# The last steps of two layers are run inside the layer that follows

## The reference

```python
x = x + mamba(_layernorm(x), ...)
x = x + ffn(_layernorm(x), ...)
x = x + attention(_layernorm(x), ...)
x = x + ffn(_layernorm(x), ...)      # the same expert weights again

# attention, per head of 8 features (16 heads), layernorm first
dist = sqrt(max(q2 + k2 - 2 * Q @ K.T, 0))
W = (SHEP_EPS + dist) ** -2
W = W / (SHEP_EPS + W.sum(-1))
out = X + (G * (W @ V)) @ W_out.T + b_out

# ffn: 16 experts, 8 of them per token, and a shared one
scores = sigmoid(x @ gate_w.T); top 8 of scores + bias, weights normalised and scaled
y = sum over experts of combine_e * ((silu(x @ w_gate_e) * (x @ w_up_e)) @ w_down_e)
y = y + (silu(x @ shared_gate_w) * (x @ shared_up_w)) @ shared_down_w
```

## Time and profile before

| | |
|---|---|
| median of 3 runs | 1519.52 us (1519.46 to 1519.74) |
| the profiled execution | 1515.65 us, span 1513.9 us |
| busy | PE 86%, DVE 84%, ACT 73%, POOL 59% of the span |
| mean granted TensorE clock | 0.899 |

### The profile page before, as it was taken

One profiled execution on the slowest core, in us unless ns is written; L12 is line 12 of the kernel. 1 busy time (PEld: TensorE's weight loads), 2 busy tenths in 40 slices (PEclk: granted clock), 3 DMA queues, 4 the chain that ended last, 5 costly groups with the idle time before them and its releaser, 6 DMA issues. The chain is left out here.

```text
span 1513.9 us, 21515 instructions
## 1 busy us (share of the span) xinstructions
PE 1302.8 (86%) x6448; PEld 636.5 (42%) x6448; DVE 1271.4 (84%) x2150; ACT 1098.4 (73%) x1594; POOL 900.4 (59%) x1054
## 2 busy tenths in 40 slices
PE   4788888998997599999997787788888579999998
PEld 3344445544553244444442233333333234444443
DVE  3999999999999988888886888888878568888885
ACT  4677877786777456556653899999999956656564
POOL 5999889989988666665665232322222026656655
PEclk8999999999999999999998677867666689999999
DMA  7122113111311043322220000000000023333331
GB/s 252 57 73 95 56 56 102 65 56 56 111 56 57 10 166 144 131 112 112 112 112 0 1 1 0 0 0 0 0 0 1 1 113 120 120 119 119 146 155 61
DMA packets 27923, 111.54 MB, mean 74 GB/s; under 512 B 4049, under 2 KB 9570, under 8 KB 19426
## 3 DMA queue, kind: packets, MB, share of 16 engines
q1 hardware_dynamic: 27010, 110.21, 19.4%
q10 hardware_dynamic: 864, 0.74, 0.2%
HBM read 108.06 MB, written 2.88 MB: 73 GB/s over the span
## 5 line engine op out<-in xcount | busy, mean ns | idle before, releaser
L1042 POOL TENSOR_TENSOR e_h_lo<-e_h,e_h_hi 128x512 f16<-128x512 f32 x272 | 314.7, 1158 | 246.4 <-ACT e_h_hi L1124 233.6
L275 POOL TENSOR_TENSOR m_h<-m_b_sb,m_dx 128x512 f32<-128x512 f32 x256 | 347.0, 1383 | 45.6 <-POOLq L67 35.8
L690 DVE TENSOR_TENSOR_SCAN m_h<-m_decay,m_h 128x1024 f32<-128x1024 f32 x112 | 255.9, 2285 | 10.9 <-DVEq L60 7.5
L393 PE MATMUL m_y_ps<-m_hc,ident 128*128 128x512 f32 x512 | 251.1, 614 | 0.0
L528 ACT ACTIVATE m_decay<-m_delta,mw_a_log 128x255 f32<-128x255 f32 x448 | 185.1, 461 | 87.7 <-DVEq L695 87.5
L1119 ACT ACTIVATE e_g<-e_g 128x512 f32<-128x512 f32 x256 | 148.9, 582 | 122.7 <-PE e_g L1064 121.5
L1124 ACT ACTIVATE e_h_hi<-e_h 128x512 f16<-128x512 f32 x272 | 169.7, 624 | 84.6 <-DVE e_h L1175 82.9
L1621 DVE TENSOR_SCALAR a_d<-a_s 128x512 f32<-128x512 f32 x256 | 170.3, 687 | 54.9 <-PE a_s L1508 35.9
L1064 PE MATMUL e_g<-ef_x_hi,ew_gate_up 128*128 128x512 f16 x544 | 207.3, 381 | 4.7 <-PEq L103 3.2
L1069 PE MATMUL e_y<-e_h_hi,ew_down 128*128 128x512 f16 x544 | 205.9, 379 | 2.1 <-POOL e_h_lo L1042 2.1
L1064 PE MATMUL e_u<-ef_x_hi,ew_gate_up 128*128 128x512 f16 x544 | 207.4, 381 | 0.0
(11 more groups left out here) (236 smaller groups left out, 2080.4 us busy)
## 6 DMA issues: line engine op xcount, KB each, us to landing
e_c_rest<-mix SPq DMA_DIRECT2D x48, 1024.0 KB, 8.7
m_b_sb<-b_rows SPq DMA_DIRECT2D x64, 512.0 KB, 5.4
ef_c_head<-mix SPq DMA_DIRECT2D x16, 1024.0 KB, 4.6
ew_gate_up<-w_gate_up SPq DMA_DIRECT2D x1, 2176.0 KB, 13.9
out<-x_sb SPq DMA_DIRECT2D x8, 256.0 KB, 2.3
ew_down<-w_down SPq DMA_DIRECT2D x1, 1088.0 KB, 11.1
mw_conv_rows<-w_conv_rows ACTq DMA_DIRECT2D x1, 640.0 KB
mix<-ef_cT SPq DMA_DIRECT2D x16, 32.0 KB, 1.6
```

The costliest lines, as they stand in the source:

```text
L275: ins = nc.gpsimd.tensor_tensor(h[:, m % 4, :, c], b_sb[:, p, 2 * m:2 * m + 2], dx[:, p, c:c + 1].to_broadcast([P, 2, T]), ALU.mult)
L393: ins = nc.tensor.matmul(y_ps[:], ident[:], hc[:, m % 2, n].rearrange("p c t -> p (c t)"), start=(m == 0 and n == 0), stop=(m == PAIRS - 1 ...
L690: nc.vector.tensor_tensor_scan(flat, decay_of(m, p)[:], flat, 0.0, ALU.mult, ALU.add).then_inc(scan_chain, 1)
L1042: nc.gpsimd.tensor_tensor(h_lo[:, k], h[:, k], h_hi[:, k], ALU.subtract).then_inc(h_lo_ready, 1)
```

## The change

At both seams the last steps of a layer move behind the barrier. `ExpertTail` holds the shared expert's h, its upper and lower half, and y; in layer 1 its last product and the addition now run in the attention's `body(-1)`, at heads 3, 6 and 9. `AttentionTail` holds what the last batch's tail needs; this tail now runs in the steps `e` = 0 to 4 of layer 3's first chunk. The two kinds of layer now share eight PSUM banks, and the first eight experts of that chunk have two banks each for gate and up. The router for this chunk moves one batch earlier (`router`), and the first expert's gate and up are made in the last batch (`first_expert`). GpSimd's norm for batch 1 moves from the attention's start into the last chunk of layer 1, and the Sqrt and Silu tables are asked for ahead. The loops of both layers keep their instructions.

```diff
+class ExpertTail:
...
+    def upper_h(self, act):
+        act.wait_ge(self.h_ready, self.STEPS + 1)
+        act.sem_inc(self.gu_free, 1)
+        self.nc.scalar.activation(self.h_hi[:], self.h[:], ACT.Copy).then_inc(self.h_hi_ready, 1)
+        act.sem_inc(self.h_ready, -(self.STEPS + 1))
+    def lower_h(self, pool):
+        pool.wait_ge(self.h_hi_ready, self.STEPS)
+        self.nc.gpsimd.tensor_tensor(self.h_lo[:], self.h[:], self.h_hi[:], ALU.subtract).then_inc(self.h_lo_ready, 1)
+        pool.sem_inc(self.h_hi_ready, -self.STEPS)
+    def down(self, pe, y):
+        pe.wait_ge(self.h_lo_ready, self.STEPS + 3)
+        for n, (r, a) in enumerate(((0, self.h_hi), (0, self.h_lo), (1, self.h_hi))):
+            ins = self.nc.tensor.matmul(y, self.ew.down[r][:, NE], a[:], start=False, stop=(n == 2))
+        ins.then_inc(self.y_ready, 1)
+        pe.sem_inc(self.h_lo_ready, -(self.STEPS + 3))
+    def read_y(self, act, y):
+        take(act, self.y_ready)
+        self.nc.scalar.activation(self.yT[:], y, ACT.Copy, scale=W_SCALE ** -2).then_inc(self.yT_ready, 1)
+    def transpose_y(self, pe, t):
+        take(pe, self.yT_ready)
+        take(pe, self.gu_free, self.STEPS + self.BANKS)
+        for tt in range(QC // P):
+            ins = self.nc.tensor.transpose(t[:, tt * P:(tt + 1) * P], self.yT[:, tt * P:(tt + 1) * P], self.ident[:])
+        ins.then_inc(self.o_ready, 1)
+    def update(self, dve, t):
+        take(dve, self.o_ready)
+        n = QC // P
+        xs = self.x_sb[:, (NQ - 1) * n:NQ * n, :]
+        self.nc.vector.tensor_tensor(xs, t.rearrange("p (a d) -> p a d", a=n), xs, ALU.add)
...
+        def banks(e, first, last):
+            few = last if nxt is not None else first and e < 8 if prev is not None else False
+            return 2 if few else BANKS
...
+                    if e < NE or not (last and nxt is not None):
+                        lower(e)
...
+                    if e > 0 or not first or prev is None:
+                        up(e, p, first, last)
+                    if first and prev is not None:
+                        prev.tensor_step(pe, e)
...
             def epilogue():
-                for n in range(3):
+                for n in range(2):
                     pe.wait_ge(h_lo_ready, STEPS + n + 1)
                     down(STEPS - 3 + n)
-                pe.sem_inc(h_lo_ready, -(STEPS + 3))
-                take(pe, yT_ready)
-                take(pe, gu_free, STEPS + BANKS)
-                transpose_y()
+                if nxt is None:
+                    rest.down(pe, y_ps)
+                    rest.transpose_y(pe, t_ps)
...
+                    if first and prev is not None:
+                        prev.vector_step(dve, e)
...
-            chunks(dve, body, lambda: None, lambda: update(NQ - 1))
+            chunks(dve, body, (lambda: prev.vector_open(dve)) if prev is not None else (lambda: None), (lambda: update(NQ - 1)) if nxt is None else (lambda: None))
...
+        if e == 12:
+            self.norm(pool)
...
+class AttentionTail:
...
+    def banks_ahead(self):
+        s, av, t, u = self.s_ps, self.av_ps, self.t_ps, self.u_ps
+        return [av[0][:], t[0][:], s[0][:]], [av[1][:], t[1][:], s[1][:]], u[:, 0:512], u[:, 512:1024]
+    def banks_behind(self):
+        s, av, t, u = self.s_ps, self.av_ps, self.t_ps, self.u_ps
+        return [s[0][:], t[0][:], u[:, 0:512]], [s[1][:], t[1][:], u[:, 512:1024]], av[0][:], av[1][:]
...
+    def vector_open(self, dve):
+        self.read_av(dve, 0)
+        self.read_av(dve, 1)
+    def tensor_step(self, pe, e):
+        if e == 1:
+            self.transpose_av(pe)
+        if e == 3:
+            self.transpose_o(pe)
+        if e == 4:
+            self.project_out(pe)
+    def vector_step(self, dve, e):
+        if e == 0:
+            self.norm_and_gate(dve, 1)
+        if e == 2:
+            self.read_oT(dve)
+        if e == 4:
+            self.update(dve, NB - 1)
...
-            body(NB - 2, 0, further=False, ahead=False)
+            body(NB - 2, 0, further=False, ahead=False, router=True)
...
             def prologue():
-                front.norm(pool)
-            def body(b, p, core=True, tail=True, heads=True, ahead=True, further=True, last=False):
-                if last:
-                    experts.norm(pool)
+                rest.lower_h(pool)
...
+                if router:
+                    experts.norm(pool)
...
+            def first_expert():
+                for side, ready in ((0, expert_sems["g_ready"]), (1, expert_sems["u_ready"])):
+                    for n, (k, x) in enumerate(((0, experts.x_hi), (0, experts.x_lo), (1, experts.x_hi))):
+                        ins = nc.tensor.matmul(s_ps[side][:], experts.ew.gate_up[k][:, 0, side], x[:, 0], start=(n == 0), stop=(n == 2))
+                    ins.then_inc(ready, 1)
...
+                    if not core:
+                        if h == 3:
+                            rest.down(pe, y_last)
+                        if h == 6:
+                            rest.transpose_y(pe, t_last)
...
+                    if router:
+                        if h == 13:
+                            experts.transpose_x(pe, t_ps[0])
+                        if h == 15:
+                            experts.route(pe, 0, t_ps[0])
                     if last:
-                        if h == 2:
-                            experts.transpose_x(pe, t_ps[0])
                         if h == 5:
-                            experts.route(pe, 0, t_ps[0])
-                    if last and h == 14:
-                        experts.transpose_comb(pe, t_ps[0])
+                            experts.transpose_comb(pe, t_ps[0])
+                        if h == 13:
+                            take(pe, s_free, 2)
+                            first_expert()
...
-                if last:
-                    experts.squash(act, t_ps[0], by_exp=True)
...
+                if router:
+                    experts.squash(act, t_ps[0], by_exp=True)
+                if last:
+                    nc.scalar.preload_act_table(ACT.Silu)
...
+            rest.upper_h(act)
+            rest.read_y(act, y_last)
+            nc.scalar.preload_act_table(ACT.Sqrt)
...
+                    if not core and h == 9:
+                        rest.update(dve, t_last)
...
+                    if router:
+                        if h == 10:
+                            experts.statistics(dve, 0)
+                        if h == 12:
+                            experts.normalise(dve, 0)
+                        if h == 14:
+                            experts.upper_x_on_vector(dve, 0, t_ps[0])
+                            experts.lower_x(dve, 0, t_ps[0])
...
+                            for part in range(3):
+                                experts.choose(dve, part, by_exp=True)
+                        if h == 5:
+                            experts.read_c_on_vector(dve, 0, t_ps[0])
```

262 lines of the change are left out of this document (131 added, 131 removed).

## The result

The changed kernel takes 1510.27 us (median of 4 runs, 1507.75 to 1511.26), the kernel before 1519.63 us beside it (1519.46 to 1520.19): ratio 0.9937 [0.9923, 0.9951]. Forecast were 1511.5 us and a range of 1507.8 to 1517.5. The profiled execution took 1507.75 us, a span of 1506.0 where 1513.9 stood before: 7.9 us less, where the sum said 8.0. One run of e7 and one of the kernel before took twice the time; medians here leave them out.

What follows compares the result with a forecast made beforehand. Bound: ScalarE through the attention, TensorE in the second experts' first chunk, with 8.6 us between where no engine is full. Seams of -4.2 and -3.8 sum to -8.0 us off the 1519.52 median: 1511.5 us, range 1507.8 to 1517.5.

Steps and rivals of the forecast that it cites:

- First seam: Experts to attention: batch 0's third Sqrt comes 4.2 us earlier, bounds 5.8 and 2.6.
- The opening: Start of the attention behind expert 15's product: 812.14 in place of 816.28, 4.14 us earlier.
- The wait for the norm: At the attention's start VectorE no longer waits 1.65 us for GpSimd's normalisation of batch 1.
- The stalls: Shared expert's matmuls and transposes among batch 0's scores add 0.9 us, from 0.0 to 2.5.
- The norm ahead of expert 12's half: GpSimd's batch 1 normalisation, moved into the first experts' last chunk, costs nothing, at most 3.0 us.
- ScalarE full to the last Exp: Through the attention ScalarE has no gap, so 4.2 us arrive at the last Exp; the squash costs 0.3.
- Start of the experts: Behind the attention's last Exp the second experts start at 1223.25 in place of 1229.99, 6.7 us earlier.
- Waits: In the second experts' first chunk TensorE waits 2.2 us before expert 3, with release 2.3 us.
- The clock: TensorE in the second experts' first chunk: staying fast costs nothing, one low stretch 1.3 us; 0.6 taken.
- Second seam: Attention to second experts: 3.8 us gained, bounds 6.7 (no waits) and 1.5.
- Round trips: Rival: stalls between TensorE and VectorE in batch 0 leave 1.0 to 2.5 us; 1514.0 us, chance 0.18.
- The low clock: Rival: TensorE stays at 1.2 GHz in the second experts' first chunk; slower, 1523 to 1540 us, chance 0.04.

Runs made afterwards that it cites:

- e7: Changed kernel, but in the second experts' first chunk GpSimd begins expert 0's lower half only when expert 1's upper half is out: 1509.16 us.
- e1: Changed kernel with only the experts-to-attention seam changed; the attention's ending and the router put back as before: 1513.07 us.
- e3: Changed kernel with batch 1's GpSimd normalisation put back first behind the experts-to-attention seam: 1511.62 us.
- e4: The changed kernel run again, unaltered, beside the others: 1507.38 us.
- e5: Changed kernel, but the tail's four gating steps on VectorE stand behind expert 2's h, and what hangs on them one step later: 1510.11 us.
- e8: e5 plus chunk 1's statistics, normalisation and GpSimd norm moved from the second experts' first chunk into the attention's last batch: 1508.77 us.

## Why the prediction was right, term by term

- *First seam, -4.2 forecast, -4.5 measured* (A in the changed kernel and in e1; over the ten traces with the whole seam -4.1 to -5.1). The opening: 4.15 us earlier against the last product, with 4.14 forecast. From the opening to the third Sqrt 21.61 us instead of 21.98, in these parts. The wait for the norm: 1.7 gone, as forecast. The addition: 0.6, forecast 0.7. The stalls: the waits of 1.07 and 0.75 cost 1.6 more than what stood there before, and 0.6 comes back because VectorE then waits less for the projection; 1.0, forecast 0.9. Two terms I had not in the sum: 0.5 for the slowed normalisation, and 0.75 won by TensorE's higher clock (0.2 in the first scores, 0.54 in the projection, whose rows before and after follow). That these nearly cancel is luck. The norm ahead of expert 12's half, priced at nothing, gains 0.43 ahead of S. Undoing the norm's move costs 2.0 to 3.0 of A by e3, not 1.65, since the wait is 1.87 there and the normalisation and TensorE's matmuls behind it are slower too.

```profile
825.54 3.78 PE L1308 MATMUL a_t<-aw_qkvg_w,af_zT 128*128 128x512 f32 x4
820.80 3.24 PE L1368 MATMUL at_t<-aw_qkvg_w,af_zT 128*128 128x512 f32 x4
```

- *ScalarE full to the last Exp:* right (380.43 of 381.40). The squash cost 0.2 in this trace, where 0.3 was forecast with 1 as the bound. The bound was too small: 2.1 us in three of the nine traces with the squash between the batches. I had summed the router's way at one clock only.
- *Start of the experts, 1.56 us behind the last Exp by the sum:* 1.58. The Trainium skill, "ScalarE: Activation LUTs", What ACT_TABLE_LOAD costs, has a drain on top of each load, about 1.38 us; the trace does not agree here either, 1.28 us and 0.28 for the seam are all there is.
- *Waits, 2.3 forecast:* 0.21 and 2.55 = 2.76. The place is right (before expert 3, released by expert 1's h); the 0.5 too much is the product's 0.7 beside GpSimd, less some of my allowances.
- *The clock, 0.6 forecast as the middle of 0 and 1.3:* 1.3 to 1.4 where it falls, 0 where not; it fell in this trace, from 1226.1 to 1229.6. That is 7.6 us into the chunk, so a sign that I had named for being wrong (0.50 beyond the first few us) did show, but for 3.5 us.
- *Second seam:* -3.8 forecast with the squash's 0.3 in it, -3.2 measured (-3.4 in C, 0.2 in B); alone and with the clock kept C falls by 4.8. The start came out as forecast, the waits 0.5 and the clock 0.7 dearer; what is left for the tail on TensorE is then some 2.0, not 2.5. The bound of -1.5 was added up wrongly: -4.4 with two low stretches (2.6) and 1 us of waits is -0.8.
- *Rivals.* Round trips did not eat the first seam; that VectorE's idle time there is all waits on TensorE was misread, since 1.65 us of it went to GpSimd's norm. The low clock came as one stretch of some 3 us, not over the chunk. That the whole tail hides did not happen: the wait before expert 3 stayed.

Sum by the yardstick: -4.5 + 0.2 - 3.4 = -7.7, with the 0.43 ahead of S -8.1; by the spans -7.9, by medians -9.4 (and -9.3 in e4). The 1.5 us between spans and medians are not explained: the profiled execution of before took 1515.65 us, less than almost all its runs, and S alone moves by 4.6 us between traces, nearly all of it in the first layer. What sets the first layer's time was not tried. By its number alone the median, 1510.27, lies midway between my 1511.5 and the 1509.0 of the rival in which all of the tail hides; the wait before expert 3 decides between them.

## What to carry to other kernels

A tail moved into the next stage is worth the hole that it leaves, less what it adds to the engine that sets the pace there: look for the order that lets the next stage's hand-over go first (e5, 0.8 us of C), and for a stage before it in which the other engine is idle (e8, 1.9 us more). Price a moved producer at both levels of TensorE's clock: a result that arrives just in time at one is 2 us late at the other. Cut traces at instructions that all kernels share, and compare the stretch, not the total, when the total spreads more than the change is worth.
